# Gathering the second layer's pass by edge tile, with TensorE reading tile slots from a table

## The reference

```python
h = relu(layernorm(x)); x = x + L0(h, ...)   # tensor-product convolution, then batch norm
h = relu(layernorm(x)); x = x + L1(h, ...)   # mean of the senders' rows, then batch norm
h = relu(layernorm(x)); x = x + L2(h, ...)   # attention with edge features
h = relu(layernorm(x)); x = x + L3(h, ...)   # attention with self loops

def L1(features, src, dst, W_src, gamma, beta):
    msgs = (features @ W_src)[src]
    rst = segment_sum(msgs, dst) / max(deg, 1) + features
    return relu(batchnorm(rst) * gamma + beta)
```

## Time and profile before

| | us |
|---|---|
| median of 3 runs (5598.19 to 5601.46) | 5600.34 |
| the profiled execution, its own time | 5590.46 |
| its span | 5588.7 |
| TensorE, VectorE, GpSimd, ScalarE busy | 3899.8, 4054.8, 3608.6, 2969.4 |
| mean clock granted to TensorE | 0.832 of full |

### The profile page before, as it was taken

The page is one execution under the profiler, slowest core; times in us unless marked ns, Lnnn a source line. Parts: engine busy times, 40 slices in busy tenths (PEclk is TensorE's granted clock), DMA queues, the critical chain, the costliest instruction groups (busy, mean ns, idle before and its releaser), DMA issues. The chain is left out here.

```text
span 5588.7 us, 88640 instructions
## 1 busy us (share of the span) xinstructions
PE 3899.8 (70%) x21179; PEld 3037.0 (54%) x21180; DVE 4054.8 (73%) x9127; ACT 2969.4 (53%) x8461; POOL 3608.6 (65%) x3623
## 2 busy tenths in 40 slices
PE   4799999999766666666684556555575566555666
PEld 3577777777545555555463455544433455454552
DVE  4799999999763333333376888888876788888887
ACT  4799999999554444444362333333343333333332
POOL 2577777777317777777607777777701777777760
PEclk9899999999877888888786777777787777777777
DMA  8444444444225455455325555555502555555543
GB/s 270 109 98 98 99 98 99 98 99 98 69 64 136 135 135 135 134 134 134 106 98 147 144 145 146 146 145 141 145 15 84 144 144 144 144 140 142 144 119 95
DMA packets 693372, 687.44 MB, mean 123 GB/s; under 512 B 458792, under 2 KB 561755, under 8 KB 691471
## 3 DMA queue, kind: packets, MB, share of 16 engines
q0 software_dynamic: 173552, 491.76, 30.9%
q1 hardware_dynamic: 378451, 164.47, 11.7%
q10 hardware_dynamic: 141276, 30.14, 2.8%
HBM read 627.87 MB, written 57.66 MB: 123 GB/s over the span
## 5 line engine op out<-in xcount | busy, mean ns | idle before, releaser
L1935 POOL DMA_INDIRECT g3rows<-sender_rows,g3idx x880 | 847.1, 963 | 515.0 <-issue 261.3
L1109 POOL DMA_INDIRECT c0rows<-rows,c0idx x880 | 994.8, 1130 | 285.2 <-issue 271.5
L1935 POOL DMA_INDIRECT g2rows<-sender_rows,g2idx x880 | 847.2, 963 | 399.3 <-issue 274.5
L878 POOL DMA_INDIRECT g1rows<-rows,g1idx x880 | 833.5, 947 | 350.4 <-issue 264.0
L999 DVE TENSOR_TENSOR acc<-acc,g1psA 128x258 f32 x660 | 279.7, 424 | 723.0 <-PE g1psA L904 568.5
L1138 ACT ACTIVATE c0z<-c0rows,c0sh 128x128 f32<-128x128 f32 x2640 | 795.3, 407 | 1.7 <-DMA c0rows<-rows,c0idx 1.7
L907 PE MATMUL g1psA<-g1rows,g1sel 128*128 128x129 f32 x2640 | 474.8, 348 | 359.0 <-DMA g1rows<-rows,g1idx 321.6
L907 PEld LDWEIGHTS g1psA<-g1rows,g1sel 128*128 128x128 f32 x2640 | 455.1, 259 | 402.1 <-issue 348.0
L1969 PE MATMUL g3psA<-g3rows,g3sel 128*128 128x136 f32 x2640 | 440.6, 327 | 157.3 <-DVE g3rows L2147 102.5
L1230 PE MATMUL c0psA<-c0prod,c0sel 128*128 128x256 f32 x1760 | 547.6, 393 | 3.5 <-DVE acc L1319 3.5
L1969 PE MATMUL g2psA<-g2rows,g2sel 128*128 128x132 f32 x2640 | 439.1, 327 | 155.0 <-DVE g2rows L2147 102.3
(11 more groups left out here) (432 smaller groups left out, 8735.0 us busy)
## 6 DMA issues: line engine op xcount, KB each, us to landing
g2bc<-dst_rows SPq DMA_DIRECT2D x55, 512.0 KB, 3.9
g3bc<-dst_rows SPq DMA_DIRECT2D x55, 512.0 KB, 3.9
g1f<-in_edge_attr SPq DMA_DIRECT2D x103, 256.0 KB, 3.5
c0rows<-rows,c0idx POOLq DMA_INDIRECT x880, 2.8
g1rows<-rows,g1idx POOLq DMA_INDIRECT x880
g2rows<-sender_rows,g2idx POOLq DMA_INDIRECT x880
g3rows<-sender_rows,g3idx POOLq DMA_INDIRECT x880
rbf_steps<-prep_extra POOLq DMA_DIRECT2D x7, 1024.0 KB, 10.7
```

The lines of the kernel that those rows point to most:

```text
L878: g.indirect_dma_start(rows[b][:, u, 0:D], None, k.table, bass.IndirectOffsetOnAxis(ap=idx[b][:, u:u + 1], axis=0)).then_inc(r_sem[b], 16)
L1109: g.indirect_dma_start(rows[b][:, m, place(n), :], None, k.table, bass.IndirectOffsetOnAxis(ap=idx[b][:, 4 * m + n:4 * m + n + 1], axis=0) ...
L1935: g.indirect_dma_start(rows[b][:, u, 0:TW], None, k.sender_rows, bass.IndirectOffsetOnAxis(ap=idx[b][:, u:u + 1], axis=0)).then_inc(gas[b] ...
```

## The change

The pass gathers each edge tile once: TB = 104 blocks of 8 tiles, 832 gathers, of which the last is of a row of zeros added to `src_tab`. They go into `ring`, 64 tiles in place of the 32 of `rows`. The indices of a block come from `src_tab` in DRAM, transposed on the way (one number to a piece). `prepare` works out and stores a table `slots` in DRAM: per step, the ring slot of its tile, and for each of the four gather semaphores the count that must be reached before that tile is there. SP loads a block's table (5 x 8 numbers) into `slot`, and TensorE reads from it 8 slots and the last step's 4 counts into registers, waits for the four counts, and multiplies out of the ring at the slots' addresses. For the first 12 blocks of steps (LEAD) it waits for the tile block of the same number instead. The steps stay 880, and so do products, one-hots and adds.

GpSimd's waits now count step blocks against tile blocks: the first half of tile block t waits for all of step block t−2, the second half for the first half of step block t−1. SP asks for the indices of tile block t when the first half of step block t−2 is done. One-hots are made one block ahead in two buffers, and `f`, `fT` and `res` have two buffers in place of four. `node_of` gets a narrower pitch. The diff, cut:

```diff
-KP = U + 16
+KP = U + 1
+R = 64
+TB = (ET + U2 - 1) // U2
+PHASES = 4
@@ prepare, SP @@
+sp.dma_start(k.src_tab[ET:ET + 1, :], zero[0:1, :].bitcast(I32)).then_inc(S["pd"], 16)
 ...
 sp.dma_start(k.heads, heads[:, :]).then_inc(S["st"], 16)
+sp.wait_ge(S["sb"], 1 + PHASES)
+for a in range(1 + PHASES):
+    sp.dma_start(k.slots[a].rearrange("(m q) -> q m", q=P), slots[:, a, :], allow_slow_non_contiguous=True
+                 ).then_inc(S["st"], 16)
@@ prepare, VectorE, behind project(FOURTH, THIRD) and ahead of the memset of heads @@
+step(nc.vector.tensor_copy(laps[:, :], laps_i[:, :]))
+for a, (per, off) in enumerate([(R, R)] + [(U2 * PHASES, U2 * b) for b in range(PHASES)]):
+    step(nc.vector.tensor_scalar(tn[:, :], tf[:, :], float(ET - 1), -float(off), ALU.min, ALU.add))
+    step(nc.vector.scalar_tensor_tensor(out=lap[:, :, :], in0=each(laps[:, :], 1, [P, Z, TB // PHASES + 1]),
+                                        scalar=float(per), in1=each(tn[:, :], 2, [P, Z, TB // PHASES + 1]),
+                                        op0=ALU.mult, op1=ALU.is_le))
+    step(nc.vector.tensor_reduce(tsum[:, :], lap[:, :, :], AX.X, ALU.add))
+    if a == 0:
+        step(nc.vector.tensor_scalar(tn[:, :], tn[:, :], float(R), None, ALU.add))
+        nc.vector.scalar_tensor_tensor(out=slots[:, a, :], in0=tsum[:, :], scalar=-float(R), in1=tn[:, :],
+                                       op0=ALU.mult, op1=ALU.add).then_inc(S["sb"], 1)
+    else:
+        nc.vector.tensor_scalar(slots[:, a, :], tsum[:, :], float(16 * U2), None, ALU.mult).then_inc(S["sb"], 1)
+    v.wait_ge(S["sb"], a + 1)
@@ aggregate, SP @@
-            def load(t, c, i, left):
-                b, n = c % 4, turns(c, i)
-                if later(n):
-                    sp.wait_ge(r_sem[b], n * per)
-                sp.dma_start(idx[b][:, :], k.src_of[:, ds(t * U2, U2)]).then_inc(i_sem[b], 16)
-                if left and later(n):
-                    sp.wait_ge(S["ha"], t - 3)
+            def load(t, b, n, left):
+                used = known(sp, t - 1) if later(n) else b - 1
+                if left and later(n):
+                    sp.wait_ge(r_sem[b], n * per)
+                reach(sp, S["ha"], used)
+                if left:
+                    sp.dma_start(idx[b][:, :], k.src_tab[ds(t * U2, U2), :].rearrange("t p -> p t"),
+                                 allow_slow_non_contiguous=True).then_inc(i_sem[b], 16)
+                sp.dma_start(slot[b][:, :, :], k.slots[:, ds(t * U2, U2)].unsqueeze(0)).then_inc(l_sem[b], 16)
+                b = b % 2
                 ...
@@ aggregate, GpSimd @@
+            def gather(t, c, n):
+                b = c % PHASES
                 g.wait_ge(i_sem[b], n * 16 + 16)
                 for u in range(U2):
                     if u % Q == 0:
-                        if later(n):
-                            g.wait_ge(S["hb" if u else "ha"], t - 1)
+                        if not isinstance(t, int) or t >= 2:
+                            g.wait_ge(S["ha"] if u else S["hb"], t if u else t - 1)
                         g.sem_inc(S["go"], 1)
-                    g.indirect_dma_start(rows[b][:, u, 0:D], None, k.table,
+                    g.indirect_dma_start(ring[:, c * U2 + u, 0:D], None, k.table,
 ...
-            eras(g, gather)
+            laps(g, gather)
@@ aggregate, TensorE @@
+                    row = wide(ring[:, ds(at[u], 1), :])
 ...
+            def slots_of(b):
+                return nc.values_load_multi_w_load_instructions(slot[b][0:1, 0, :], engines=[PE], ...)[1]
+            def needs_of(b):
+                return [pe.value_load(slot[b][0:1, 1 + q, U2 - 1:U2], min_val=per, max_val=TB * per) for q in range(PHASES)]
+            def rows_in(t, b, need):
+                if isinstance(t, int) and t < LEAD:
+                    pe.wait_ge(r_sem[b], (t // PHASES + 1) * per)
+                    return
+                for q in range(PHASES):
+                    pe.wait_ge(r_sem[q], need[q])
+            def multiply(t, b, n, left):
+                pe.wait_ge(l_sem[b], n * 16 + 16)
                 if left:
+                    turn(t, b % 2, twos(n, b))
+                at = slots_of(b)
+                need = None if isinstance(t, int) and t < LEAD else needs_of(b)
                 pe.wait_ge(S["sel"], t + 1)
-                pe.wait_ge(r_sem[b], n * per + per)
+                rows_in(t, b, need)
                 ...
@@ aggregate, ScalarE: in body, one_hot(t + 1) goes ahead of leave(t); before, one_hot(t + 2) stood behind it @@
```

More of the change, by code:

```diff
@@ L811, in aggregate @@
         HALF = W // 2
[L812 to L820, removed]
+        NF = TB
+        LAP = R // U2
+        LEAD = 3 * PHASES
+        idx = [sb(f"idx{b}", [P, U2], I32) for b in range(PHASES)]
+        slot = [sb(f"slot{b}", [1, 1 + PHASES, U2], I32) for b in range(PHASES)]
+        ring = sb("ring", [P, R, W])
+        sel = [sb(f"sel{b}", [P, U2, P]) for b in range(2)]
+        f = [sb(f"f{b}", [P, EU, C]) for b in range(2)]
+        fT = sb("fT", [P, 2, EU // 2 * P])
+        res = sb("res", [2 * H, 2, EU // 2, P])
+        we, av = ring[:, R - 2, 0:D], ring[:, R - 1, 0:D]
         fold = sb("fold", [P, H])
@@ L826, in aggregate, with twos, eras, laps @@
         block = es.enter_context(nc.Block())
-        f_sem, e_sem = [S[f"lf{b}"] for b in range(4)], [S[f"es{b}"] for b in range(4)]
-        i_sem, r_sem = [S[f"idx{b}"] for b in range(4)], [S[f"gat{b}"] for b in range(4)]
+        f_sem, e_sem = ([S[n + str(b)] for b in range(2)] for n in ("lf", "es"))
+        l_sem, i_sem, r_sem = ([S[n + str(b)] for b in range(PHASES)] for n in ("sl", "idx", "gat"))
         per = 16 * U2
[L830 to L844, removed]
+        def twos(n, b):
+            return n * 2 + b // 2
+        def eras(eng, body, lead=PHASES):
+            for t in range(lead):
+                body(t, t % PHASES, t // PHASES, True)
+            with eng.Fori(lead // PHASES, (NF - 1) // PHASES) as i:
+                for b in range(PHASES):
+                    body(i * PHASES + b, b, i, True)
+            for t in range((NF - 1) // PHASES * PHASES, NB2):
+                body(t, t % PHASES, t // PHASES, t < NF)
+        def laps(eng, body):
+            for t in range(LAP):
+                body(t, t, t // PHASES)
+            with eng.Fori(1, TB // LAP) as i:
+                for c in range(LAP):
+                    body(i * LAP + c, c, i * (LAP // PHASES) + c // PHASES)
+            for t in range(TB // LAP * LAP, TB):
+                body(t, t % LAP, t // PHASES)
         @block.sync
@@ L902, in sums @@
                     u = half * Q + n
+                    row = wide(ring[:, ds(at[u], 1), :])
                     if n == 3:
-                        ins = nc.tensor.matmul(to[:, 2, 0:W], sel[b][:, u, :], rows[b][:, u, :], start=True, stop=True)
+                        ins = nc.tensor.matmul(to[:, 2, 0:W], sel[b % 2][:, u, :], row, start=True, stop=True)
                         continue
                     for o in range(2):
-                        ins = nc.tensor.matmul(to[:, o, n * HALF:(n + 1) * HALF], sel[b][:, u, :],
-                                               rows[b][:, u, o * HALF:(o + 1) * HALF], start=True, stop=True)
@@ L909, in sums @@
-                return ins
-            def multiply(t, c, i, left):
-                b, n = c % 4, turns(c, i)
+                        ins = nc.tensor.matmul(to[:, o, n * HALF:(n + 1) * HALF], sel[b % 2][:, u, :],
+                                               row[:, o * HALF:(o + 1) * HALF], start=True, stop=True)
+                return ins
+            def slots_of(b):
+                return nc.values_load_multi_w_load_instructions(
+                    slot[b][0:1, 0, :], engines=[PE], min_val=0, max_val=R - 1,
+                    skip_runtime_bounds_check_because="made in prepare() as remainders of R")[1]
@@ L952, in one_hot, with body @@
                                      ).then_inc(S["sel"], 1)
-            def body(t, c, i, left):
+            def body(t, b, n, left):
+                if not (isinstance(t, int) and t >= NB2 - 1):
+                    one_hot(t + 1, (b + 1) % 2)
                 if left:
-                    leave(t, c % 4, turns(c, i))
-                if not (isinstance(t, int) and t >= NB2 - 2):
-                    one_hot(t + 2, (c + 2) % 4)
+                    leave(t, b % 2, n)
                 if not isinstance(t, int) or 1 <= t <= NF:
-                    result(t - 1, (c - 1) % 4, turns(c, i) - (1 if c % 4 == 0 else 0))
+                    result(t - 1, (b - 1) % 2, twos(n, b) - (1 if b % 2 == 0 else 0))
             one_hot(0, 0)
-            one_hot(1, 1)
             eras(a, body)
-            for b in range(4):
-                a.wait_ge(e_sem[b], 16 * (NF // 4))
+            for b in range(2):
+                a.wait_ge(e_sem[b], 16 * (NF // 2))
         @block.vector
         def _(v):
-            for b in range(4):
```

(10 more changed lines are left out.)

61 lines of the change are left out of this document (33 added, 28 removed).

## The result

The changed kernel takes 5780.6 us in the median (5776.5 to 5784.3, four runs) against 5599.3 (5594.9 to 5601.5, four runs): 1.0325 times as long, 95% interval 1.0307 to 1.0343. The prediction was 5551: it was wrong by 230 us, and on the wrong side.

A forecast was written before the change was run, and what follows sets the result against it. The second layer's pass was taken as bound by GpSimd's 880 gathers. Gathers −60.1, start +1.2, early blocks +7 and end +3 gave −49 us, 5541.5, or 5551 us carried to the median; range 5538 to 5585, forecast's own 5540 to 5562.

The forecast's parts named there:

- The change part by part: The prediction's list of priced parts, from gathers to preparation, against the profiled 5590.46 us; sum −49 us.
- the new index load: Pass start: first gather waits for 1024 pieces of 4 bytes from DRAM; run time between nothing and 6.6 us, total +1.2.
- The preparation's stores: Behind `heads`, SP issues five more stores of 896 pieces, 1.2 us each, until 135; next stage begins at 158: 0.
- Gathers: Second layer's pass: 832 gathers instead of 880, 1.252 us each, −60.1 us if GpSimd never waits for long.
- Early blocks: First 18 or so blocks of the pass, where new waits bind: 10.4 us a block instead of 10.02, +7 us.
- TensorE's new reads: Table reads of 8 values and four of 1 per block: 0.8 to 2.0 us, taken 1.4, covered, 0 on the path.
- Index loads: Rival: in early blocks index loads take 6.6 us instead of 3.1, +28 instead of +7, 5572 us; chance 0.07.
- the start: The pass's first gather waits for the index load from DRAM in 4-byte pieces: +1.2 us.
- the end: After the pass's last gather TensorE may be behind, between 0 and 8.6 us; taken as +3 us.
- its four cases that end faster: Forecast 0.72, late index loads 0.07, second-half wait all along 0.06, preparation not covered 0.08; faster given 0.89.
- the rivals: TensorE the bound 0.07, late index loads 0.07, second-half wait binding all along 0.06, preparation not covered 0.08.
- TensorE as the bound: Rival: second layer's table reads and address operations do not pass beside products; pass 72 us longer, 5672 us; chance 0.07.

The follow-up runs named there:

- pitch 20: The changed kernel with node_of's pitch (KP) at 20 values (80 bytes) instead of 17 (68 bytes): 5557.9 us, 0.9933 of before.

## Why the prediction was wrong

*The step that failed first is one that is not in it.* The change part by part goes from the gathers to the preparation and leaves out `KP`. The diff shows it, the prediction prices nothing for it, and it is 214 of the 230 us. The rows for it were there: the earlier trace rows has a read of 16 values at 1.107 us on TensorE's queue, in a loop that the change does not rewrite but whose operand it moves. That the place of a read matters no row of before shows (every read there started on a multiple of 16); but a range from both sides, such as the prediction draws for the new index load, was not drawn for it.

*The price of a read was taken from one kind of place.* The Trainium skill (Runtime: NRT & Kernel Launch, Instruction fetch mechanics) gives about 200 ns per register even in bulk; it says this of register loads that the runtime adds to a program, and the reads here are the kernel's own, out of SBUF. The trace's 69 ns a value spoke against it, and for the aligned reads that stands. The reads that do not start on a multiple of 16 took 3.80 us for 16 values, 238 ns each: that is near the Trainium skill's figure, but no run here shows that the reason is the same. I took the row for the price of such reads altogether, when it was the price at the places that it had. For the reads that the change adds it was right: 0.60 and 0.30 us.

*The preparation's stores were priced at their issue.* "SP issues five more stores of 896 pieces, 1.2 us each, until 135; the next stage begins at 158: 0." The issue was even shorter, 0.57 each. What it left out is what 4480 pieces of 4 bytes then do to the stores of 896 and 1024 KB that the stage's end waits for: +16.3 us to the stage's end in this profile. Of these 1.9 were there ahead of the stores (`heads` issued at 130.64 instead of 128.79) and are not the change's: with pitch 20 and the same operations it was issued at 128.89. The pieces and the large stores go through the same 16 DMA engines in queues of their own; why the large ones stay slow after the last piece, the runs do not show. The Trainium skill (DMA: Bandwidth & Descriptors, Rules for kernel authors) says that a non-contiguous last dimension becomes one descriptor per element. The trace agrees: between 130 and 150 us SP's queue has 4626 packets, and 6 in the kernel before. I bounded how long such pieces run for the new index load, and not for these.

*The rest held.* Gathers: 832, each still 1.25 us apart (688 from 1882.0 to 2740.7). Early blocks: 144 gathers from 1692.0 to 1880.8 are 9.8 us over that pace; +7 was forecast. GpSimd's waits for TensorE in the pass:

```profile
L922 POOL DMA_INDIRECT g1ring<-rows,g1idx x832 | 786.6, 945 | 346.3 <-issue 245.2 <-DMA g1idx<-src_tab 83.8 <-PE g1psA L949 14.5
```

14.5 us (3.7 before), 13.3 of it in the first 144 gathers, as forecast. TensorE's new reads cost 0.60 and four times 0.30, 1.8 us a block where I took 1.4 within 0.8 to 2.0; a register operation of 0.15 behind each single one, which I left out, makes it 2.4. They stayed off the path: TensorE was not the bound. Index loads were not late (83.8 us of waiting, 82.5 before, the start of the pass in both). With the two failed steps taken out, the kernel measures 5551.3 and 5550.8, 44 and 43 us under before where −49 was forecast. That it comes so near is in part luck: the early blocks cost 9.8 us and not 7, the start 0.7 and not 1.2 (6.1 us from the stage's first load to the first gather, 5.4 before), and the end gave 1.6 back where I had it lose 3 (8.4 us from the last gather to the last product, 10.0 before). These terms come to −51, and where the other 7 or 8 us lie is not settled; the stretch behind the last gather alone differs by 6.5 between two profiles of one kernel.

Two sums and one reading of the prediction are off, without bearing on what failed. Its range, by its own terms, is 5541 to 5566 (−60.1 + 1.2, and −60.1 + 1.2 + 16 + 8.6), not 5540 to 5562; and its four cases that end faster add up to 0.93, not 0.89. GpSimd's 75.6 to 75.7 us busy in a hundred are 75.8 in the pass's first hundred.

None of the rivals was the cause. The one that I gave the other side, TensorE as the bound by its table reads, had the right engine and the right instruction, in the wrong pass.

## What to carry to other kernels

List every line of the diff before pricing any, constants first: a pitch or an order that many loops read is an edit in each of them. For a table read into registers, keep each row's start on a multiple of 16 bytes, and look at which engine's queue reads it with no running operation to cover the read. A transfer's price is its issue, its time in the DMA engines, and what it slows there.

## What the runs showed of the hardware

A read of 16 values into registers took 1.10 us from a multiple of 16 bytes and 3.6 to 3.8 from any other place, on TensorE's queue and on VectorE's. Each store of 896 pieces of 4 bytes put off the next stage, which waited for large stores, by 2 to 3 us (10 to 15 for five of them), and ten such stores kept SP's queue issuing for 39.37 us where five took 3.28. On VectorE 2.5 us more in each block's read, under a product that ran on, cost 0.1%.
